# Nine stack copies of a batch move from SyncE's queue to GpSimd's

## The reference

```
qkv = x @ c_attn_w + c_attn_b                  # 16 heads of 8 features
s   = q k^T / sqrt(8), causal; p = softmax(s)
heads 0, 1, 2: p *= 1.6 in one third of the keys, renormalised
x1  = layernorm(x + (p v) @ c_proj_w + c_proj_b)
h   = s0 * [x1, -x1] @ (+-1 from k0); h = 2 relu(h)      # 512 wide
h   = s1 * h @ (+-1 from k1);         h = 2 relu(h)      # 512 wide
out = layernorm(x1 + s2 * h @ (+-1 from k2))
```

## Time and profile before

| | us |
|---|---|
| median of 3 runs | 1004.72 |
| lowest, highest | 1001.64, 1010.22 |
| the profiled execution | 1005.2 |
| its span in the profile | 1003.3 |

### The profile page before, as it was taken

One profiled execution on the slowest core, in us unless ns is written; L12 is line 12 of the kernel. 1 busy time (PEld: TensorE's weight loads), 2 busy tenths in 40 slices (PEclk: granted clock), 3 DMA queues, 4 the chain that ended last, 5 costly groups with the idle time before them and its releaser, 6 DMA issues.

```text
span 1003.3 us, 18215 instructions
## 1 busy us (share of the span) xinstructions
PE 901.3 (90%) x6848; PEld 502.5 (50%) x6848; DVE 671.5 (67%) x1752; ACT 604.2 (60%) x1106; POOL 438.2 (44%) x505
## 2 busy tenths in 40 slices
PE   2349799999999999999999999999999999999866
PEld 1125344555555554555555554655565554645343
DVE  2255668586877868586877868585867869685334
ACT  2105557576666757576766757576766767476733
POOL 1102334545454554545454554535554554435430
PEclk9657999999999999999999999999999999999887
DMA  3654545345353535445353525454353525300000
GB/s 77 67 68 60 66 54 65 53 61 68 42 68 41 74 39 75 52 63 67 44 66 42 75 40 75 50 65 65 49 64 43 73 30 75 39 23 2 23 10 10
DMA packets 66141, 53.23 MB, mean 53 GB/s; under 512 B 4519, under 2 KB 64007, under 8 KB 66055
## 3 DMA queue, kind: packets, MB, share of 16 engines
q1 hardware_dynamic: 65190, 51.30, 40.2%
q10 hardware_dynamic: 864, 0.79, 0.3%
HBM read 9.24 MB, written 4.19 MB: 13 GB/s over the span
## 4 chain that ended last, share of the span: by engine, by line
PE 63%; ACT 18%; DVE 7%; DMA 5%; issue 2%; SPq 2%; POOL 1%; ACTq 1%; POOLq 0%; DVEq 0%
PE av_ps L875 11%; PE max_ps L816 10%; PE score_ps L842 10%; PE bank_ps L902 7%; PE bank_ps L903 7%; ACT e L513 6%; PE bank_ps L799 4%; ACT res L531 4%; PE max_ps L818 4%; PE bank_ps L948 3%; DVE h_hi L717 3%; ACT full L505 2%; DMA stack<-negmaxT 2%; DMA stack<-parts 2%; PE bank_ps L937 2%
## 5 line engine op out<-in xcount | busy, mean ns | idle before, releaser
L513 ACT ACTIVATE e<-score_ps 128x512 f32<-128x512 f32 x640 | 370.5, 597 | 210.4 <-PE score_ps L842 207.6
L816 PE MATMUL max_ps<-stack 72*128 72x512 bf16 (+3 forms) x1024 | 277.6, 311 | 31.4 <-DMA stack<-parts 24.1
L842 PE MATMUL score_ps<-stack 75*128 75x512 bf16 (+3 forms) x1024 | 247.1, 303 | 24.5 <-DMA stack<-negmaxT 16.7
L638 DVE TENSOR_REDUCE negmax<-max_ps 128x1 f32<-128x512 f32 x256 | 170.2, 684 | 127.9 <-PE max_ps L818 127.6
L422 POOL TENSOR_SCALAR_AFFINE_SELECT e<-e 128x512 f32<-128x512 f32 x256 | 162.8, 656 | 139.2 <-ACT e L513 139.2
L429 POOL TENSOR_TENSOR h_lo<-full,h_hi 128x512 fp32r<-128x512 f32 x120 | 155.1, 1297 | 112.4 <-DVE h_hi L717 112.4
L816 PEld LDWEIGHTS max_ps<-stack 72*128 72x128 bf16 x1024 | 101.8, 99 | 192.0 <-issue 73.4
L818 PE MATMUL max_ps<-ident_bf,future_bf 128*128 128x128 bf16 x1024 | 197.4, 224 | 0.0
L875 PE MATMUL av_ps<-e,vaug 128*9 128x512 f32 (+3 forms) x2048 | 187.4, 438 | 2.1 <-ACT avT L520 1.9
L641 DVE TENSOR_REDUCE negmax<-max_ps 128x1 f32<-128x384 f32 x256 | 140.3, 548 | 47.4 <-PE max_ps L818 47.0
L505 ACT ACTIVATE full<-bank_ps,scales 128x512 f32<-128x512 f32 x128 | 86.6, 688 | 99.9 <-PE bank_ps L903 97.0
(11 more groups left out here) (86 smaller groups left out, 945.8 us busy)
## 6 DMA issues: line engine op xcount, KB each, us to landing
stack<-parts SPq DMA_DIRECT2D x288, 128.0 KB
x_in<-in_L_attn_hidden_states SPq DMA_DIRECT2D x16, 256.0 KB, 4.8
x_res<-in_L_attn_hidden_states SPq DMA_DIRECT2D x16, 256.0 KB, 11.0
out_x<-res SPq DMA_DIRECT2D x16, 256.0 KB, 10.3
stack<-negmaxT ACTq DMA_DIRECT2D x32, 24.0 KB
e<-in_L_ffn_k SPq DMA_DIRECT2D x1, 256.0 KB, 3.1
wc<-in_L_attn_c_attn_w SPq DMA_DIRECT2D x1, 192.0 KB
e<-in_L_ffn_k SPq DMA_DIRECT2D x1, 128.0 KB, 3.2
```

Source lines behind the costliest of these rows:

```text
L513: nc.scalar.activation(e[g % 2][:, t, :], score_ps[:, t % 2, :], ACT.Exp, scale=SCALE).then_inc(exped, 1)
L638: ins = nc.vector.reduce_max(negmax[:, half, 3, h + t:h + t + 1], buf, AX.X, negate=True)
L816: nc.tensor.matmul(out_ap[:, col:col + width], st[0:QK_ROWS, h, 0, P * qt:P * qt + P], st[0:QK_ROWS, h, 1, 0:width], start=True, stop=False)
L842: return nc.tensor.matmul(out_ap[:, col:col + width], st[0:ALL_ROWS, h, 1, P * kt:P * kt + P], st[0:ALL_ROWS, h, 0, P * kt:S], start=True, ...
```

## The change

The copies of half 1 (heads 8 to 15) of every batch, batch 0 included, are issued by GpSimd, as the first thing of its iteration n for batch n+1, behind the same two waits. SyncE keeps half 0 and everything else.

```diff
@@ sync @@
-            def later_half(n):
-                b = n + 1
-                if not live(b) or (b.c == 0):
-                    return
-                sp.wait_ge(split_step, b.times(3, 3))
-                if live(n + -1):
-                    sp.wait_ge(scored, (n + -1).times(G * STEPS, 4 * STEPS))
-                stack_half(b, 1)
-
             def earlier_half(n):
...
                     stack_half(b, 0, levels=(2,))
-                    stack_half(b, 1)
                     return
...
             def iteration(n):
-                later_half(n)
                 b = n + 3
@@ gpsimd @@
+            def later_half(n):
+                b = n + 1
+                if not live(b):
+                    return
+                pool.wait_ge(split_step, b.times(3, 3))
+                if live(n + -1):
+                    pool.wait_ge(scored, (n + -1).times(G * STEPS, 4 * STEPS))
+                for a in range(3):
+                    for c in range(3):
+                        row = R * (3 * a + c)
+                        nc.gpsimd.dma_start(stack[b.parity][row:row + R, HALF:H, :, :],
+                                            parts[b.parity][64:P, c:3 + a + 1:3 + a - c, :]
+                                            ).then_inc(stacked[b.parity][1], 16)
+
             def iteration(n):
...
+                later_half(n)
                 masks(0, 0)
                 low(1, 0)
                 low(1, 1)
```

## The result

| | before | after |
|---|---|---|
| median, us (4 runs each) | 1007.24 | 1018.31 |
| lowest to highest | 1001.64 to 1010.22 | 1015.25 to 1021.20 |
| profiled execution | 1005.2 | 1016.2 |
| its span | 1003.3 | 1014.3 |

The ratio is 1.0116, with a 95% interval of 1.0082 to 1.0150. Run again later beside other kernels it was 1.0107 (1.0068 to 1.0146). The change costs 11 us. I had forecast 47: the sign is right, the size is four times too large, and it is made up of other parts. Executions of the kernel before ranged from 1001.2 to 1011.9 us in all, so 2 or 3 us can be told from medians only, and one execution each of experiments 1 and 10 took over 4600 us: the ratios leave it out, the medians given there (1007.34, 1009.50) do not and would be 1007.06 and 1008.24 without it.

What follows compares the result with a forecast made beforehand. The prediction took transfers to bound the start and TensorE the steady part. It summed 1005.2 (profiled execution) + 44 (13 steady iterations) + 3 (start) = 1052 us, range 1003 to 1125.

Steps and rivals of the forecast that it cites:

- What bounds the kernel: Whole program: transfers bound the start (17 to 58 us), TensorE the steady part, busy 54.37 of 56 us a batch.
- The path of the delay: Steady iterations: GpSimd's copies delay the low part, then ScalarE's third eviction and exponential, then TensorE's score; 3.4 us each.
- held time less 6.99 us: TensorE's loss in each of 13 steady iterations: 9c - 6.99 us, nothing below c = 0.78.
- The price of c: Time one copy holds GpSimd: SyncE's 0.66 us times 1.74, from a subtraction on VectorE and GpSimd, 1.15 us.
- 44 us: Steady term: TensorE loses 3.4 us in each of 13 iterations that have layer 1 tiles and a next batch.
- rival 1: Steady iterations: the copies hide in the slack, 0 to 10 us lost, some 1007 us; chance 17%.
- The ratio in the Trainium skill: Cross-check: first byte about 1 us from GpSimd, 0.6 from SyncE; would give c 1.1 us, sum 38 us.
- The start: Batch 0's second half issued by GpSimd beside the first: taken as +3 us, between +6.4 and -10.
- Both of its cases: Start: half of GpSimd's transfers meet SyncE's eight transfer engines, +6.4 us; or they meet the idle eight, -10.
- Rival 3, the clock: Steady iterations: each new TensorE stall also lowers the clock, 2.0 us each, 26 us more, 1078 us; chance 20%.
- Rival 2, faster by the start: Start: idle transfer engines take GpSimd's copies, waits of 3.0 and 10.1 us go, 992 us; chance 5%.
- All three signs of being wrong: c outside 0.9 to 1.4, ScalarE's wait not passing to TensorE, or the start moving by over 10 us.

Runs made afterwards that it cites:

- experiment 1: Changed kernel with only batch 0's half 1 copies given back to SyncE: 1007.34 us, ratio 1.0033 to the kernel before.
- experiment 10: Kernel before, but SyncE issues batch 1's copies only once batch 0's first maxima rows have landed: 1009.50 us, ratio 1.0036.
- experiment 7: Kernel before, no copies on GpSimd, with six powers (6.09 us) put in the copies' place on GpSimd: 1006.00 us, ratio 1.0009.
- experiment 2: Changed kernel, but GpSimd issues only batch 0's half 1 and SyncE all other copies: 1012.89 us, ratio 1.0088 to the kernel before.
- experiment 3: Changed kernel, but GpSimd waits until batch 0's first half has landed before issuing its second: 1008.03 us, ratio 1.0027 to the kernel before.
- experiment 9: Changed kernel with batch 0's half 1 on SyncE and GpSimd's copies moved behind the residual's bias: 1016.10 us, ratio 1.0102 to the kernel before.
- experiment 8: Kernel before, but GpSimd issues four of the nine copies of each half of batches 0 and 1: 1004.84 us, ratio 0.9992.
- experiment 11: Kernel before, batch 1's copies held for batch 0's first maxima rows, batch 0's half 1 by GpSimd once half 0 landed: 1007.18 us, ratio 1.0024.
- experiment 5: Changed kernel with four powers (4.06 us) behind GpSimd's nine copies in iterations 2 to 14: 1076.54 us, ratio 1.0694 to the kernel before.

## Why the prediction was wrong, point by point

- **What bounds the kernel:** right, with a limit. The start is bound by transfers, the steady part by TensorE. But the start was bound by how fast one queue moved, 62 GB/s: with two the engines moved 111.
- **The path of the delay** (GpSimd's copies, low part, eviction, exponential, score): right, to the instruction. The formula "held time less 6.99 us" gives 3.23, 5.76 and 7.12 us where TensorE's rows have 3.23, 5.78 and 7.10, and experiment 7 shows no loss at 5.8.
- **The price of c: this step failed.** I took 1.15 us, by the ratio in which GpSimd is slower than VectorE in a subtraction. It is 0.70 us, SyncE's own 0.66 within 7%. The ratio of the two engines in an elementwise loop did not carry over to issuing. Because the cost is a step, the error was not of 40% but of the whole term: 9 x 0.70 = 6.3 lies under 6.99, and 44 us became about 1 us (what the traces gain over the 13 iterations). The lower end of my range was the right value and had 17% as rival 1.
- **The ratio in the Trainium skill,** page "DMA: Bandwidth & Descriptors" (Specifications), about 1 us to the first byte from GpSimd for about 0.6 us from SyncE, gave an estimated c of 1.1 us. Taken as a measure of holding time it is not borne out: the measured ratio is 0.70 to 0.66. The page speaks of the first byte, which no run here shows.
- **The start: also mis-sized.** +3 us forecast, with an upper bound of +6.4; it is about 8 us in the runs (experiment 2: 0.9%) and 11 in the trace. The first half lands 11.2 us later where I allowed 9.4 and then averaged that away. Both of its cases came true at once: GpSimd's copies used what had been idle (a transfer share of 1.11 for 0.57), and SyncE's were held back all the same. By experiment 3, the delay of the first half is GpSimd's copies beside it. By which of the sixteen engines the copies ran stays open. I also left out that the later maxima rows queue beside more copies (8.90 for 6.63 us).
- **The residue:** GpSimd's other 135 copies cost 0.3% (0.15 to 0.52). ScalarE's longer waits are there in experiment 7 too, at no cost, and experiment 9 did not decide. The traces of experiments 1 and 2 put most of it in the start, in the waits for copies and maxima rows of the first batches, and about 1 us in the 13 iterations, most of it in the last (836.82 to 889.53 before, 848.52 to 902.10 after: 0.9 us). There TensorE waits 0.7 us for VectorE's maxima, which it did not before, so VectorE's slower casts are a candidate. No run moved only the copies of batches 1 and 2 back to SyncE, so this is read from traces and not tested.
- **Rival 3, the clock:** did not happen in the changed kernel, which has no stall, but does as soon as there is one, at 1.5 to 2.1 us for each. I gave it 20%; with the forecast's own c it would have come.
- **Rival 2, faster by the start:** out. Experiments 8, 10 and 11 moved the start's waits about and won nothing beyond their intervals.

All three signs of being wrong that the prediction named came: c lies outside 0.9 to 1.4, ScalarE's wait does not pass on to TensorE, and the start moved by 11 us. Had GpSimd been held 10.22 us, a c of 1.14, the changed kernel would have stood at 1076 us, as experiment 5 shows, and not at 1052. The sum that came nearest to the truth was the one for rival 1, plus a start costed by its worst case. That the sign is right is partly luck: the steady term that carried it is nearly nothing, and the start, forecast at 3 us, gave the 11.

## What to carry to other kernels

Work out the slack that stands before a cost first, and then ask only whether the cost lies under it: near such a step, a price that is off by 60% decides everything, so state the cases and not a mean. Take the price of an engine's DMA issue from another queue's issue, not from its arithmetic. A second queue can raise what moves in all and still hurt: here copies that used to stand behind an urgent set and now ran beside it delayed that set by 11 us, so ask first what must land first. And a stall of TensorE may cost more than its length, as the clock may fall with it.

## What the runs showed that was not expected

- A DMA issued by GpSimd held it 0.70 us in this kernel, 64 KB or 128 KB alike (12.87 us for eighteen, 6.43 for nine).
- A DMA of 24 KB on three partitions took 3 us alone (experiment 10) and 12.8 us beside queued copies of 128 KB.
- Eighteen copies on two queues moved 111 GB/s where one queue moved 62, and yet the nine that were needed first landed 11.2 us later.
- A stall of TensorE of 3.2 us was enough to bring the granted clock to 0.75 in the mean of the 7 us around its end and behind it, but not in every iteration: from 343.5 to 403.4 us in experiment 5 it stayed at 1.00, and the period was 59.9 instead of 61.1 us.
